# Input tiles loaded by one transfer each, the shifted ones from GpSimd's queue, with a new order of small products on TensorE

## The reference

```python
def _L0_conv_ref(x, W, b, y):
    mean_feat = jnp.mean(x, axis=(1, 2))
    offsets = jnp.clip(mean_feat @ W + b, 0, 28).astype(jnp.int32)
    ...
    # the image shifted down by dy and right by dx, zeros where nothing comes from
    gathered = x[bidx, ci[:, :, None], cj[:, None, :], :]
    return jnp.where(mask, gathered, 0)
# _L1_conv_ref: 3x3 convolution of the signs of x with the summed signs of W, plus b
# _L2, _L3: cosine transform along one axis, Fourier transform along the other,
#           32 x 32 modes mixed over the channels, transformed back, plus x @ W.T + b, then relu
x = x + _L0_conv_ref(_gn(x), L0_conv_W, L0_conv_b, 224)
x = x + _L1_conv_ref(_gn(x), L1_conv_W, L1_conv_b)
x = x + _L2_conv_ref(_gn(x), ...)
x = x + _L3_conv_ref(_gn(x), ...)
```

## Time and profile before

| | us |
|---|---|
| runs, median of 3 | 3735.57 |
| lowest, highest | 3716.77, 3765.04 |
| the profiled execution | 3730.91 |
| its span | 3729.1 |
| busy in the span: PE | 3021.7 (81%) |
| DVE | 2734.8 (73%) |
| ACT | 1510.7 (41%) |
| POOL | 38.0 (1%) |

### The profile page before, as it was taken

How to read it: one execution, slowest core, us unless ns; L and a number is a source line. 1 busy time by engine, 2 the same in 40 slices (tenths; PEclk the granted TensorE clock), 3 DMA queues, 4 the chain that set the end, 5 groups by cost and what they waited for, 6 DMA issues and landing times. The chain is left out here.

```text
span 3729.1 us, 58608 instructions
## 1 busy us (share of the span) xinstructions
PE 3021.7 (81%) x17264; PEld 1399.1 (38%) x17264; DVE 2734.8 (73%) x3908; ACT 1510.7 (41%) x2728; POOL 38.0 (1%) x35
## 2 busy tenths in 40 slices
PE   0188888888888888898937988888898827999997
PEld 0033343333444334344426433333333306444443
DVE  3888777778787777887523677776867643999998
ACT  3466765566665566665443322222222223000000
POOL 0000000000000000000010000000000010000000
PEclk9988887788787778889976999999999867999998
DMA  4677655667565666665364746556465355999998
GB/s 147 174 219 213 199 183 170 192 196 216 175 192 180 190 197 201 195 194 166 122 142 144 287 197 241 227 214 256 186 261 205 144 118 149 341 389 392 377 382 302
DMA packets 272198, 808.67 MB, mean 217 GB/s; under 512 B 85466, under 2 KB 119774, under 8 KB 261108
## 3 DMA queue, kind: packets, MB, share of 16 engines
q1 hardware_dynamic: 212948, 488.15, 41.2%
q10 hardware_dynamic: 58368, 316.72, 21.9%
q0 software_dynamic: 608, 0.63, 0.1%
HBM read 479.39 MB, written 329.56 MB: 217 GB/s over the span
## 5 line engine op out<-in xcount | busy, mean ns | idle before, releaser
L1425 ACT ACTIVATE B_junk<-B_im,B_nk 128x896 bf16<-128x896 f32 x224 | 232.8, 1039 | 718.0 <-DVE B_im L1483 583.2
L470 PE MATMUL A_cps<-A_sign,A_cfull 128*128 128x448 bf16 x1344 | 421.9, 399 | 12.2 <-issue 8.9
L1676 PE MATMUL C_ring<-C_im,C_wnorm 128*128 128x448 f32 x896 | 387.7, 571 | 23.2 <-DVE C_ubuf L1733 17.7
L498 PE MATMUL A_aps<-a_k_ident,A_image 128*112 128x128 f32 x1792 | 289.0, 308 | 134.3 <-DVE A_image L838 112.4
L1371 PE MATMUL B_ring<-B_im,B_wnorm 128*128 128x448 f32 x896 | 385.1, 571 | 7.0 <-DVE B_wnorm L1454 4.8
L612 ACT ACTIVATE A_tout<-A_aps 112x512 f32<-112x512 f32 x448 | 248.3, 591 | 350.1 <-PE A_aps L498 349.6
L475 PE MATMUL A_cps<-A_sign,A_cedge 32*32 32x448 bf16 x1344 | 379.7, 392 | 0.0
L477 PE MATMUL A_cps<-A_sign,A_cedge 32*32 32x448 bf16 x1344 | 379.2, 392 | 0.2 <-issue 0.2
L1343 PE MATMUL B_ring<-B_rout,b_k_rowf 128*64 128x512 f32 x896 | 279.4, 707 | 118.4 <-DVE B_rout L1476 118.4
L838 DVE SCALAR_TENSOR_TENSOR A_image<-A_cps,A_cbias,A_image 128x896 f32<-128x896 f32 x224 | 256.7, 1146 | 156.6 <-PE A_cps L470 153.3
L1483 DVE SCALAR_TENSOR_TENSOR B_im<-B_ring,B_im 128x896 f32<-128x896 f32 x224 | 239.0, 1084 | 175.4 <-PE B_ring L1381 173.8
(11 more groups left out here) (196 smaller groups left out, 3472.1 us busy)
## 6 DMA issues: line engine op xcount, KB each, us to landing
A_rin<-in_x SPq DMA_DIRECT2D x2016, 112.0 KB, 2.4
x2s<-A_image ACTq DMA_DIRECT2D x112, 896.0 KB, 4.8
B_im<-x2s SPq DMA_DIRECT2D x112, 896.0 KB, 9.6
x3s<-B_im ACTq DMA_DIRECT2D x112, 896.0 KB
C_im<-x3s SPq DMA_DIRECT2D x112, 896.0 KB, 11.9
out<-C_rout ACTq DMA_DIRECT2D x192, 256.0 KB
out<-C_rout ACTq DMA_DIRECT2D x192, 192.0 KB
out<-C_rout ACTq DMA_DIRECT2D x64, 128.0 KB
```

Of the source, the lines that this page charges most:

```text
L470: return nc.tensor.matmul(banks[:, s, 0:LPN], cfull[:, tap, :], lines(n, s, slice(0, P), 0, tap), start=(tap == 0), stop=(tap == 2), skip_ ...
L498: last = nc.tensor.transpose(aps[side][0:HR, l * P:(l + 1) * P], image[q][:, first:first + 2 * HR].rearrange("p (j s) -> p s j", s=2)[:, l ...
L1676: nc.tensor.matmul(slot(add_place(e))[:, lane % 2, 0:2 * SIZE], wnorm[par][:], im[par][:, EVN * e:EVN * (e + 1)].rearrange("p (m s) -> p s ...
```

## The change

Each tile is loaded by one transfer whose source has the dimensions i (4), l (32) and the row, and whose destination is all 128 partitions. x tiles and shifted tiles have semaphores of their own for each ring buffer (`x_in`, `s_in`), which count 16 a tile. The shifted tiles, with the wait for the offsets and the loads of the two registers, go from SP's queue to GpSimd's, which runs a loop over the images of its own. On PE, `statistics` 3 moves from slot 0 of the next body, where it stood behind the first convolution, to the end of slot 15, and `forward_cols` 5 moves in slot 13 from ahead of `turn_back` 12 to behind `statistics` 2 of the image after.

```diff
-        in_full = [sem(f"in_full{i}") for i in range(RING)]
+        x_in = [sem(f"x_in{i}") for i in range(RING)]
+        s_in = [sem(f"s_in{i}") for i in range(RING)]
...
+        def load(queue, done, flat, k, slot):
+            rows = flat.rearrange("(l i q) c -> i l (q c)", i=QG, q=SIZE)
+            first = (k % 8) * CHQ
+            queue.dma_start(rin[slot][:, :], rows[:, :, first * C:(first + CHQ) * C]).then_inc(done[slot], 16)
...
-            def load(flat, k, slot):
-                rows = flat.rearrange("(l f) c -> l (f c)", l=32)
-                for i in range(QG):
-                    first = i * SIZE + (k % 8) * CHQ
-                    sp.dma_start(rin[slot][32 * i:32 * i + 32, :],
-                                 rows[:, first * C:(first + CHQ) * C]).then_inc(in_full[slot], 16)
...
             def body(b, has_x, has_tail):
-                back = None
                 for s in range(SLOTS):
                     for k in x_tiles(s) if has_x else ():
                         sp.wait_ge(tile_turned, tile_no(b, x_at(k)) - RING + 1)
                         sp.sem_inc(off_seen, 1)
                         load_x(b + 2, k, x_at(k) % RING)
-                    for k in s_tiles(s):
-                        if k == 0:
-                            sp.wait_ge(off_ready, b + 2)
...
-                        sp.wait_ge(tile_turned, tile_no(b, s_at(k, has_x)) - RING + 1)
-                        sp.sem_inc(off_seen, 1)
-                        load_shifted(b + 1, k, s_at(k, has_x) % RING, back)
...
                     if has_v and s < UNITS:
                         conv(b, s)
-                    if has_v and has_s and s == 0:
-                        statistics(b, 3)
                     if has_tail and s < 5:
                         spectrum(b - 1, 2 * s, ring_base(b))
-                    if has_v and s >= 3 and s % 2 == 1:
+                    if has_v and s in (3, 5, 7, 9, 11):
                         forward_cols(b, q, (s - 3) // 2)
...
                     if has_x and s in (12, 13):
                         statistics(b + 1, s - 11)
+                    if has_v and s == 13:
+                        forward_cols(b, q, 5)
                     if has_s and s == 13:
                         statistics(b, 4)
+                    if has_v and s == 15:
+                        forward_cols(b, q, 6)
+                    if has_x and s == 15:
+                        statistics(b + 1, 3)
...
+            pool.wait_ge(pad_done, 16 * (SIZE * C // BANK + 1))
+
+            def body(b, has_x):
+                back = None
+                for s in range(SLOTS):
+                    for k in s_tiles(s):
+                        if k == 0:
+                            pool.wait_ge(off_ready, b + 2)
+                            pool.sem_inc(pool_seen, 1)
+                            dy = pool.value_load(offi[0:1, 0:1], min_val=0, max_val=MAXOFF)
+                            dx = pool.value_load(offi[0:1, 1:2], min_val=0, max_val=MAXOFF)
+                            back = dy * SIZE + dx
+                            pool.sem_inc(off_taken, 1)
+                        pool.wait_ge(tile_turned, tile_no(b, s_at(k, has_x)) - RING + 1)
+                        pool.sem_inc(pool_seen, 1)
+                        load_shifted(b + 1, k, s_at(k, has_x) % RING, back)
```

More of the change, by code:

```diff
@@ L217, in shift_conv_forward @@
         off_seen = sem("off_seen")
+        pool_seen = sem("pool_seen")
         off_taken = sem("off_taken")
@@ L273, in tile_no, with x_loaded, s_loaded @@
             return TILES + 2 * TILES * (b + 1) + at
-        def tile_loaded(b, at):
-            return 64 * (2 * TILES // RING * b + 3 * TILES // RING + at // RING + 1)
+        X_AT = [x_at(k) for k in range(TILES)]
+        S_AT = [s_at(k, True) for k in range(TILES)]
+        def x_loaded(b, at):
+            slot = at % RING
+            per = sum(t % RING == slot for t in X_AT)
+            return 16 * (TILES // RING + per * (b + 1) + sum(t % RING == slot for t in X_AT if t <= at))
+        def s_loaded(b, at, has_x):
+            slot = at % RING
+            per = sum(t % RING == slot for t in S_AT)
+            here = S_AT if has_x else range(TILES)
+            return 16 * (per * (b + 1) + sum(t % RING == slot for t in here if t <= at))
         def stat_tiles(s):
@@ L354, in _ @@
                          x[0, 0:P].rearrange("r q c -> r (q c)")).then_inc(pad_done, 16)
-            def load(flat, k, slot):
-                rows = flat.rearrange("(l f) c -> l (f c)", l=32)
-                for i in range(QG):
-                    first = i * SIZE + (k % 8) * CHQ
-                    sp.dma_start(rin[slot][32 * i:32 * i + 32, :],
-                                 rows[:, first * C:(first + CHQ) * C]).then_inc(in_full[slot], 16)
-            def load_x(b, k, slot):
[L364 to L370, removed]
+            def load_x(b, k, slot):
+                load(sp, x_in, x_pix[bass.ds(b * (SIZE * SIZE) + (k // 8) * (QG * SECOND * SIZE), P * SIZE), :], k, slot)
             def store_spec(b):
@@ L803, in turn_x, with add_shifted @@
                 t, ch = divmod(k, 8)
-                dve.wait_ge(in_full[slot], loaded)
+                dve.wait_ge(x_in[slot], loaded)
                 nc.vector.transpose(turned_view(image[q], SECOND * t, ch * CHQ, CHQ),
                                     flat_view(rin[slot][:, :])).then_inc(tile_turned, 1)
-            def add_shifted(b, q, k, at_tile):
+            def add_shifted(b, q, k, at_tile, has_x):
                 t, ch = divmod(k, 8)
@@ L884, in _ @@
                     dve.wait_ge(junk_done, junk_x(0, ("square", k - 8)) + 1)
-                turn_x(0, k, k % RING, 64 * (k // RING + 1))
+                turn_x(0, k, k % RING, 16 * (k // RING + 1))
                 if k == 0:
@@ L914, in body @@
                     for k in s_tiles(s) if has_s else ():
[L915 removed]
+                        add_shifted(b, nxt, k, s_at(k, has_x), has_x)
                     if has_s and s == 12:
@@ L955, in _, with load_shifted @@
             pool.dma_start(b0s[:], b0[None, :].to_broadcast([P, 2])).then_inc(wload, 16)
+            def load_shifted(b, k, slot, back):
+                if isinstance(b, int) and b == 0 and k < 8:
+                    load(pool, s_in, pad_pix[bass.ds(29 * SIZE - back, P * SIZE), :], k, slot)
+                else:
+                    load(pool, s_in, x_pix[bass.ds(b * (SIZE * SIZE) + (k // 8) * (QG * SECOND * SIZE) - back, P * SIZE), :], k, slot)
+            pool.wait_ge(pad_done, 16 * (SIZE * C // BANK + 1))
[13 more added lines that the diff above has]
+                        load_shifted(b + 1, k, s_at(k, has_x) % RING, back)
+            body(-1, True)
+            body(0, True)
+            with pool.Fori(0, (NB - 4) // 3) as i:
+                for k in range(3):
+                    body(3 * i + 1 + k, True)
+            body(NB - 3, True)
+            body(NB - 2, False)
 def mix_modes(nc, NB, rre, rim, wt, bb, con, statm, gscale, spec, mixed, tag):
```

10 lines of the change are left out of this document (2 added, 8 removed).

## The result

| | before | after |
|---|---|---|
| median of 4 runs each, us | 3727.28 | 4168.44 |
| lowest, highest | 3716.77, 3765.04 | 4153.98, 4182.54 |
| the profiled execution | 3730.91 | 4176.66 |
| its span | 3729.1 | 4175.0 |

A forecast was written before the change was run, and what follows sets the result against it. The prediction took a tight PE and DVE exchange as the bound, then four full DMA engines: per image +21 - 4.7 + 4 = +20 us, fifteen times +300, prologue +46, giving 4077 us from 3731; range 3670 to 4450.

The forecast's parts named there:

- The bound and the four engines: First stage: PE and DVE both near full; merged tiles, outermost count 4, run on four of 16 DMA engines, +21 us per image.
- the signs named in advance: Changed profile: prologue DMA share near 0.25, tile steps 4.6 to 5.9 us, period 130 us, PE under 80% busy.
- Price of a tile: Loading one merged tile on four engines: 4.6 us at 25 GB/s, 5.9 at 19.4; 5.2 taken.
- Hence the prologue: First x tile at 55.9 us as before, the other 15 at 5.2 us instead of 1.93: +46 us once.
- The stretch of x tiles: Image loop, while x tiles are loaded and turned: from about 74 us to 95, bounds of growth 9 to 33.
- The order on PE: Image loop: moving two PE products saves 4.7 us per image, bounded by 0 and 7.8.
- GpSimd's queue: +4 forecast: Image loop: shifted tiles issued by GpSimd land later, +4 us per image, bounds -2 and +8.
- so most of the 10 us is hidden: Shifted tiles on GpSimd's queue: four ring places, 10 to 14 us, cover their lateness except for an image's first tile.
- The last two bodies: End of the first stage, where no x tiles are loaded: 0 us change.
- B: Rival for the image loop: four engines, but hidden, period stays 112 us; 3710 to 3790 us, chance 0.08.
- C: Rival for merged tiles: all 16 engines share each; 3640 us, from 3600 to 3730, chance 0.18.
- D: Rival for all merged transfers: shifted ones too on the same four engines, 163 us per image; about 4540 us, chance 0.08.

The follow-up runs named there:

- e6_halves: The changed kernel with each tile in two transfers of 64 rows, outermost count 2; run once, 5160.26 us.
- e2_merged_sp: The changed kernel, merged tiles and new order kept, with the shifted tiles back on SP's queue; 4657.65 us, 1.253 of the kernel before.
- e4_flat: The changed kernel with the source's 128 rows outermost instead of 4, so rows fill other partitions and the output differs; 3663.23 us, 0.986 of the kernel before.
- e8_swap: The changed kernel with queues exchanged: merged x tiles on GpSimd's, merged shifted tiles on SP's; 4324.01 us, 1.159 of the kernel before.
- e3_order: The kernel before, four transfers a tile all on SP's queue, with only the new PE order and separate semaphores; 3745.92 us, 1.005 of before.
- e9_stat3: The kernel before with only `statistics` 3 moved to the end of slot 15; 3765.20 us, 1.008 of before.
- e12_queue: The kernel before, four transfers a tile and old order, with only GpSimd's queue for shifted tiles and separate semaphores; 3717.27 us, 0.998 of before.
- e5_flat_sp: e4_flat with the shifted tiles back on SP's queue; 3662.64 us, 0.983 of the kernel before.
- e7_x_four: The changed kernel with x tiles in four transfers on SP's queue, shifted tiles still merged on GpSimd's; 4078.50 us, 1.091 of the kernel before.
- e1_four: The changed kernel with four transfers of 32 rows a tile again, GpSimd's queue and new order kept; 3737.38 us, 1.005 of the kernel before.

## Why the prediction was right, and where it was not

**The bound and the four engines: right, and shown.** The step on which the forecast turned, "if the split goes by the outermost counts of both sides", holds at 2, 4 and 128 (e6_halves, e2_merged_sp, e4_flat), and 505 us come and go with it. The Trainium skill's rule (DMA: Bandwidth & Descriptors, Why a DMA increments its semaphore by 16 and not by 1), the largest number up to 16 that divides both outermost sizes, fits all four points, its fixed engines on SP's queue fit e2_merged_sp, and its changing groups on GpSimd's fit the shares of 0.76 and 0.47 in e8_swap.

Most of the signs named in advance are there: a prologue share of 0.26, a period of about 130 us with PE busy 77% of it (100.13 of 130), x tiles as DVE's largest wait, none for the offsets' product, 10.3 us on GpSimd's queue. The step of 4.37 us lies a little under the 4.6 to 5.9 named, and the landing on SP's queue isn't given by the profile.

**Price of a tile: 4.6 to 5.9 us, measured 4.37** in the prologue. I took the busy rate of the loop (19.4 GB/s) for the upper end and a value between; nearest was the one row of a single engine at work, 25 GB/s, and even that was a little low (26.2). Hence the prologue: +36.7 where I had +46, and +37 for 4.6 us. The first tile came at 58.95, not 55.9, 3 us that I had not counted.

**The stretch of x tiles: 95 forecast, 99.4 measured** (from 74 to 95, +21; measured from 74.0 to 99.4, +25.4). The mechanism was that one: the rise of DVE's wait for x tiles, 25.5 us, is nearly the whole of the rise. The size isn't clean evidence for my sum, though: see the errors below.

**The order on PE: -4.7 forecast, 0 measured with four transfers a tile.** The step that failed is "the first removes DVE's 4.7 us wait". It did remove that wait (2.0 us in the whole trace, where it was 68.7), and I took it for a gain of the period. e3_order shows the same time as a wait for the convolution: PE does the same work in front of the same next convolution, and DVE needs both. I should have asked what PE does instead. For the 0.5 and 0.8% that e3_order and e9_stat3 lose, I have no cause. No run has merged tiles in the old order, so what the order is worth in the changed kernel is open; there the waits for convolutions did not grow (8.0 to 3.5), and the shorter tail would fit a gain of about 5.

**GpSimd's queue: +4 forecast; 0 or +21, by the transfer.** With small transfers it costs nothing (e12_queue, 0.998), with merged ones on sixteen engines nothing either (e4_flat against e5_flat_sp). There the landing was 3.5 us and not the 5.2 to 5.4 of the earlier trace rows; rows of cold weight loads in the prologue were a poor measure. With merged tiles on four engines the 10 us that I had worked out were right (10.3), and "so most of the 10 us is hidden" was wrong: e7_x_four pays 23.3 us per image over e1_four for them alone. Against the period of before (108.5) it is +21.0. The first tile of an image is part of it: I had it 2 to 6 us late, and it comes 5.2 later in the mean (8.0 to 13.2; 9.3 in the image shown). The 10 us were also put together from two wrong parts: less landing than I took, and more for the four engines (last section).

**The errors and the sum.** 21 + 4 - 4.7 = 20 a period was forecast, 25.8 measured over all fifteen. 3.5 of that gap are the base: I took 112 us for every period before, where the mean of the fifteen is 108.5. In the images of the table the period rises from 112.7 to 133.7, by 21.0. The total was 4077 against 4176.66 in the profiled execution: 100 us too little, 86 of them in the fifteen periods, 19 in the last two bodies, 4 behind the first stage, less 9 in the prologue. That 20 comes so near 21.0 is in part luck, as terms of the wrong size stand in it. By the runs the parts would be 25.4 for the merged x tiles or 21 for the merged shifted ones; together they cost 25.8, not 46. Both fill places of the same ring of four, and while DVE waits for an x tile, the shifted tile behind it has time to land: after the change DVE waits 7.0 us in the stretch for shifted tiles, in e7_x_four 20.9. So x tiles were the last to come, as forecast, but with x tiles fast the shifted ones would have taken their place at nearly the same period. That overlap is read from waits. Merged x tiles beside small shifted ones weren't run, and why the tail of e7_x_four (37.4) is longer than that of the changed kernel (29.6) stays open.

**The last two bodies: 0 forecast, +18.8 measured.** They load no x tiles, but the last but one still adds the merged shifted tiles of image 15. I had priced the four engines on x tiles alone.

**The rule of the Trainium skill against GpSimd's queue** (SBUF — State Buffer, Who interferes with whom). If a hold of GpSimd's writing while DVE runs in a two-port mode fell into an issue, it would stretch it. The trace of the changed kernel has its issues of merged tiles (ns min/median/max) at one length, whatever DVE does:

```profile
L364 POOL DMA_DIRECT2D A_rin<-in_x x248: 679/679/688, 214.4 to 2221.6; - x124
```

So nothing of the up to 9 us per image is seen in the issues. A hold outside them would be part of the landing, but in the prologue of e8_swap a tile takes 10 us too, and no `signs` instruction runs there.

**The rivals.** B (hidden) fell to the period of 134. C is what the kernel does with sixteen engines: e4_flat has 3663 where C said 3640, and its bounds of 3600 to 3730 hold it. D is e2_merged_sp: 164.3 us per image where D said 163, 4658 where it said 4540. Two thirds of that gap are again the base of 112 instead of 108.5 and the 1.3 us more per image (73 us in all), and 35 are the last two bodies (226.9 us, 191.7 before).

## What to carry to other kernels

Before merging transfers, look at the outermost count of the pattern that is left: here 4 instead of 32 took twelve of sixteen engines away, and all that merging gave on sixteen engines was 74 us (e4_flat against e1_four), where on four it cost 431 (the changed kernel against e1_four). A share of DMA time near 1/16, 2/16 or 4/16 in a stretch where transfers of one kind run alone tells this from a single row of a profile. A wait that is removed by moving a product ahead on a busy engine is no gain until one has named what that engine now does later, and who waits for that.

## What the runs showed of the hardware

- **A transfer on four engines lands later on GpSimd's queue than its bytes explain.** With sixteen engines a tile lands in 4.6 us there and in 4.2 on SP's (e4_flat). On four engines it needs 4.37 us of their time at the pace of SP's queue in the prologue, on sixteen a quarter of that, 1.1, so I would expect 4.6 + 3.3 = 7.9 us; it is 10.3. The trace's record of every packet has most of the rest. A tile is 64 packets of 7168 B, so 16 for each of four engines. In the loop such a packet takes 401 ns in the mean in the changed kernel, 358 in e4_flat, and 413 in e8_swap from 67 to 85 us, where only x tiles move; two pieces of 3584 B on SP's queue take 280 in the prologue. If the packets of one engine follow each other, that is 16 x 0.401 = 6.4 us instead of 4.37, and with 4 x 0.358 = 1.4 in e4_flat the estimate is 4.6 - 1.4 + 6.4 = 9.6 us. Why a packet takes longer there is open.
- **A transfer on four engines has 192 extra packets on GpSimd's queue.** The queue's count (packets, MB, share) is 70240 after the change and 21088 in e4_flat for the same 256 tiles, the first eight from `xpad` included. The difference, 49152, is 192 a tile, and all of them carry 8 B and take 9 ns: 12 x 16, which would be sixteen for each of the twelve engines without data. e6_halves fits: 448 a tile, 2 x 14 x 16 for its two transfers on two engines each. They are too short to explain the landing.

```profile
q0 software_dynamic: 70240, 118.48, 10.9%
```

- **PE's granted clock was lower in the kernel in which it waited more.** For the same products of the first stage PE was busy 1515.5 us before and 1638.4 after, at a mean granted clock of 0.85 and 0.81. With 2.4 GHz as 1 and 1.2 GHz as 0.5, that is 30% and 38% of the time at the lower level. Ahead of it lies more idle time: 385 us of the stage before, 702 after.

The rows of the stage, before and after:

```profile
0.00:1900.00 1900.00, 1515.51 (x8404) 690.55 (x8404) 1407.38 (x2574) 1145.34 (x2176) 5.30 (x11) 0.85 0.60 184
...
0.00:2340.00 2340.00, 1638.44 (x8402) 736.00 (x8403) 1408.15 (x2574) 1157.24 (x2176) 179.24 (x267) 0.81 0.47 149
```

In e2_merged_sp, with its longer waits, an image stands at 0.70 and 112.4 us of PE. Nothing here shows that the 123 us by which PE's busy time grew cost time of the whole: PE's idle time grew too, and its largest wait is for DVE.
